# Weaving the output projection of a batch into the next batch's features, first q/k/v projection and score maxima (Trainium2, one core)

## The reference

```python
adj = emb_s * emb_t * softmax(x) / sqrt(n)        # diagonal -inf
x = x + (one where adj is among the 10240 largest of a batch, else zero)
scale, shift = split(cond @ W_emb + b_emb)
xn = rmsnorm(x) * g_norm * (1 + scale) + shift
q, k, v = split(xn @ W_qkv)                       # 16 heads of 64
q, k = rmsnorm(q) * g_q, rmsnorm(k) * g_k
o = softmax(q @ k.T / 8) @ v
x = x + o + o @ W_out
```

## Time and profile before

| | us |
|---|---|
| three runs | 4087.24, 4088.06, 4086.60 (median 4087.24) |
| the profiled execution | 4087.43, of which span 4085.7 |
| PE busy in the span | 3797.2 (93%) |
| DVE, ACT, POOL busy | 2589.9, 1545.2, 1283.3 |
| first A\|B boundary, last values matmul of the batch to the first pair of the next | 1165.88 to 1389.43 |
| the same work in the start, without an old batch | 287.35 to about 450 (features, q/k/v, maxima) |

### The profile page before, as it was taken

The page is one execution under the profiler, slowest core; times in us unless marked ns, Lnnn a source line. Parts: engine busy times, 40 slices in busy tenths (PEclk is TensorE's granted clock), DMA queues, the critical chain, the costliest instruction groups (busy, mean ns, idle before and its releaser), DMA issues.

```text
span 4085.7 us, 44416 instructions
## 1 busy us (share of the span) xinstructions
PE 3797.2 (93%) x16035; PEld 2457.0 (60%) x16035; DVE 2589.9 (63%) x4521; ACT 1545.2 (38%) x2727; POOL 1283.3 (31%) x1907
## 2 busy tenths in 40 slices
PE   5885899999988899999989899999989899999999
PEld 2334666666644667766644677777644677666744
DVE  8996777777774777777774677777775322322221
ACT  1005444444423444444422444444432344444430
POOL 1005433333303533333312533333312433333310
PEclk9996899999998899999999799999999799999999
DMA  4002010000134000010024100000124100000023
GB/s 156 0 15 103 16 37 21 21 21 21 34 133 147 16 21 21 27 31 21 21 101 154 55 21 21 21 21 21 37 71 161 31 21 21 21 21 21 21 81 99
DMA packets 179360, 195.25 MB, mean 48 GB/s; under 512 B 7576, under 2 KB 137680, under 8 KB 178128
## 3 DMA queue, kind: packets, MB, share of 16 engines
q1 hardware_dynamic: 179152, 192.55, 14.9%
HBM read 144.29 MB, written 48.23 MB: 47 GB/s over the span
## 4 chain that ended last, share of the span: by engine, by line
PE 73%; DVE 14%; ACT 5%; POOL 4%; issue 3%; DMA 1%; SPq 0%; DVEq 0%; POOLq 0%; ACTq 0%
PE pax L1003 24%; PE ppv L1072 18%; PE pst L1058 10%; PE pst L991 10%; PE pax L1038 7%; DVE mx L823 3%; DVE xr L718 3%; DVE trash L683 3%; PE pax L1021 2%; POOL xn L379 1%; PE pax L1046 1%; PE pax L1096 1%; ACT sA L545 1%; ACT pt L552 1%; DVE otok L838 1%
## 5 line engine op out<-in xcount | busy, mean ns | idle before, releaser
L1003 PE MATMUL pax<-wh,xn 128*128 128x384 f32 x3840 | 1058.1, 347 | 11.8 <-issue 8.8
L1072 PE MATMUL ppv<-pt,v 128*65 128x512 f32 x2048 | 987.8, 594 | 1.0 <-DVE otok L838 1.0
L683 DVE TENSOR_SCALAR_CACHE_REDUCE trash<-keys,state 128x2048 uint8<-128x2048 f32 x384 | 899.8, 2343 | 9.9
L823 DVE TENSOR_REDUCE mx<-pax 128x1 f32<-128x512 f32 x960 | 617.9, 685 | 222.6 <-PE pax L1038 202.2
L1003 PEld LDWEIGHTS pax<-wh,xn 128*128 128x128 f32 x3840 | 704.7, 189 | 22.9 <-issue 19.6
L552 ACT ACTIVATE pt<-pst 128x1024 f32<-128x1024 f32 x512 | 524.5, 1024 | 503.9 <-PE pst L1058 445.7
L1003 PE MATMUL pax<-wl,xn 128*128 128x384 f32 x1920 | 649.3, 338 | 0.0
L809 DVE TENSOR_REDUCE ss<-sq 128x4 f32<-128x256 f32 x256 | 107.2, 419 | 782.2 <-ACT sq L527 782.2
L1038 PE MATMUL pax<-sA 65*128 65x512 f32 x960 | 473.3, 540 | 28.3 <-ACT sA L540 17.5
L1072 PEld LDWEIGHTS ppv<-pt,v 128*65 128x65 f32 x2048 | 278.5, 137 | 297.2 <-issue 221.7
L351 POOL TENSOR_TENSOR wl<-wf,wh 128x1024 fp32r<-128x1024 f32 x99 | 235.9, 2387 | 586.1 <-ACT wh L468 586.1
(11 more groups left out here) (139 smaller groups left out, 4445.0 us busy)
## 6 DMA issues: line engine op xcount, KB each, us to landing
wf<-in_L_cond_W_qkv SPq DMA_DIRECT2D x99, 512.0 KB, 5.4
keys<-in_x SPq DMA_DIRECT2D x32, 512.0 KB, 8.9
xin<-in_x SPq DMA_DIRECT2D x32, 512.0 KB, 4.0
out_x<-xin SPq DMA_DIRECT2D x32, 512.0 KB, 2.6
wo<-in_L_cond_W_out SPq DMA_DIRECT2D x4, 4096.0 KB, 13.6
pt<-out_x SPq DMA_DIRECT2D x64, 256.0 KB, 3.9
out_x<-pt SPq DMA_DIRECT2D x64, 256.0 KB, 2.5
oT_scr<-ostg SPq DMA_DIRECT2D x56, 256.0 KB, 2.0
```

Source lines behind the costliest of these rows:

```text
L683: e.tensor_scalar(trash[:], kv, thr_f, None, ALU.is_ge, ALU.add, accum_out=cnt[:, c:c + 1]).then_inc(z_cnt, 1)
L823: e.tensor_reduce(mx2[:, j // T, j % T, c:c + 1], max_banks(alone, j)[:, c, :], axis=AX, op=ALU.max).then_inc(m_mx, 1)
L1003: i = e.matmul(qkv_bank(alone, t)[:, 0:6 * DH], xn[:, a, k, t * P:(t + 1) * P], w[:, k, :, :].rearrange("p s c -> p (s c)"), start=(k == 0 ...
L1072: i = e.matmul(ppv[0:DH + 1, c, :], v2[:, par, kt, hh, :], pt[:, kt % 2, c * HALF:(c + 1) * HALF], start=(kt == 0), stop=(kt == T - 1))
```

## The change

- The 16 halves of the projection become calls `project(b, q, lo, hi)` that stand between other work of PE: `last_head` puts q0 to q2 (but for the last head) around the turns of the last head; q3 to q6; q7 one matmul at a time in the first `features`; q8, q9 around the first q/k/v tile; q10 in the second `features`; q11, q12; q13 before the last transposes; q14 and q15 one matmul at a time between the groups of `score_max`. `prep_alone` is gone: all engines run its steps inside `boundary`.
- DVE takes one add per tile beside `finalise_tile` instead of two, and normalises the last head between the ties. Features of rows 512 to 1023 are interleaved with the first two q/k/v tiles.
- `wo`, `xin`, `xr`, `eqm`, `scn` exist twice, by the side of the batch (`side(b)`), and the pair's sides of `sA`, `sB`, `v2` are `(i + b) % 2`, in place of `i % 2`. `xtmp` becomes `xfull`, which holds all columns and shares its place with `xn[:, 1]` (the low part is written over the full one). The halves of `xfull` that are free hold the heads of tiles 0 to 3 until the features reach them; tiles 4 to 7 go to `v2` of the side or to `heads_t`, which now has 128 partitions.
- Row 64 of `sA` is set to -1 once per side and batch (`minus_row`), and is no longer zeroed for each pair: `score_max` contracts over `0:DH`, 64 rows.
- DVE's conditioning in the first boundary comes after its tile 2 instead of 4, and ACT copies the rows of it after its first tile instead of its fourth.
- SP loads the new x first, then the residual; a batch's keys are loaded after all its predecessor's tiles are stored, and the second pair's weights after half 12.

```diff
-    xtmp = sb("xtmp", [P, 2, HALF])
-    wo = sb("wo", [P, KT, N])
...
+    wo = [inner.enter_context(nc.sbuf_tensor(f"wo{r}", [P, KT, N], F32)) for r in range(2)]
...
+    xfull = inner.enter_context(nc.sbuf_tensor("xfull", [P, KT, N], F32))
...
+    xin, xr, eqm, scn = [], [], [], []
+    for r in range(2):
+        xin.append(sb(f"xin{r}", [P, 2, N]))
+        xr.append(sb(f"xr{r}", [P, 4, N]))
+        eqm.append(sb(f"eqm{r}", [P, N]))
+        scn.append(sb(f"scn{r}", [P, N]))
...
+    def side(b):
+
+        return b % 2 if b else 1
...
-    def heads_of(k, t):
-
-        return ostg[:, t * P:(t + 1) * P] if k == KT - 1 else oTt[:, t % 2, k, :]
+    early = xfull[:, 0:KT - 1, HALF:N]
+
+    def late(b, t):
+
+        at = heads_t[:] if t % 2 else v2[:, b % 2].rearrange("p t h d -> p (t h d)")
+        return at[:, 0:(KT - 1) * P].rearrange("p (k c) -> p k c", c=P)
+
+    def heads_of(b, k, t):
+
+        if k == KT - 1:
+            return ostg[:, t * P:(t + 1) * P]
+        return early[:, k, t * P:(t + 1) * P] if t < 4 else late(b, t)[:, k, :]
 
     CST = 2
...
+                e.wait_ge(t_pv, CST + T * 2 * PAIRS * (ob + 1))
+            if fb is not None:
+                self.x_tile(fb, 0)
+                self.x_tile(fb, 1)
...
+                    if t == 1:
+                        self.store_half(ob, 0)
+                    if t > 0:
+                        self.store_half(ob, t)
+            if kb is not None:
+                if ob is not None:
+                    e.wait_ge(t_ot, 2 * PAIRS * (ob + 1))
+                self.load_keys(kb)
...
+                e.dma_start(wo[b % 2][:], w_out.rearrange("(k p) n -> p k n", p=P)).then_inc(d_wo, 16)
+                e.wait_ge(a_qkv, T * PAIRS * (b + 1))
+                e.wait_ge(d_ost, 32 * (PAIRS - 1) * (b + 1) + 16)
+                e.dma_start(early, oT_pairs[:, 0:KT - 1, 0:HALF]).then_inc(d_oe, 16)
+                self.heads_tile(b, 4)
 
...
+
+            e, cols = self.e, slice(g * HALF, (g + 1) * HALF)
+            e.wait_ge(f_ev, 2 * KT * b + KT * g + k + 1)
+            e.tensor_tensor(xn[:, 1, k, cols], xfull[:, k, cols], xn[:, 0, k, cols].bitcast(F32),
+                            ALU.subtract).then_inc(f_lo, 1)
...
+            gp = PAIRS * fb
+            for t in range(4):
+                self.feature_scale(fb, t)
+            for k in range(KT):
+                self.feature_low(fb, 0, k)
+            for t in range(4, 7):
+                self.feature_scale(fb, t)
+            self.prep_tile(gp, 0)
+            self.feature_scale(fb, 7)
+            self.prep_tile(gp, 1)
+            for k in range(KT):
+                self.feature_low(fb, 1, k)
+            self.minus_row(fb, fb % 2)
...
+        def minus_row(self, b, par):
+            e.memset(sA[par][DH:DH + 1, 2:4, :].bitcast(F32), -1.0).then_inc(a_row, 1)
...
             for t in range(T):
-                if fb is not None:
-                    self.finalise_tile(fb, t)
-                    if ob is None and t == T // 2:
-                        self.conditioning()
-                if ob is not None:
-                    self.project_tile(ob, t)
-            if fb is not None:
-                for j in range(2):
-                    e.wait_ge(d_x1[j], 16 * (T // 2) * (fb + 1))
+                self.finalise_tile(fb, t)
+                if ob is None and t == 2:
+                    self.conditioning()
+                if t == 1:
+                    self.add_half(ob, 0)
+                if t > 0:
+                    self.add_half(ob, t)
+            self.add_half(ob, 8)
+            self.prep_sums(gp, 0)
+            self.prep_split(gp, 0)
+            self.add_half(ob, 9)
...
+            self.add_half(ob, 13)
+            self.prep_split(gp, T - 1)
+            for j in range(2 * T):
+                self.row_max(gp, j, True)
+                if j in (6, 13):
+                    self.add_half(ob, 14 + (j > 6))
...
+        def last_head(self, ob, fb):
+
+            e, gp = self.e, PAIRS * ob + PAIRS - 1
+            e.wait_ge(o_wi, ob + 1)
+            e.wait_ge(d_oe, 16 * (ob + 1))
+            self.project(ob, 0, 0, 4)
+            self.out_tokens(gp, 1)
+            self.project(ob, 0, 4, 7)
+            self.project(ob, 1, 0, 7)
+            self.out_rows(gp, 0)
+            if fb is not None:
+                self.before(fb)
+            self.project(ob, 2, 0, 4)
+            self.out_rows(gp, 1)
+            self.project(ob, 2, 4, 7)
+            e.wait_ge(t_oe, 2 * PAIRS * (ob + 1))
+            for q in range(3):
+                self.project(ob, q, 7, 8)
-                    self.project_tile(ob, t, 0)
-                if fb is not None and t == 0:
-                    self.before(fb)
-                    if ob is None:
-                        self.conditioning()
-                if ob is not None:
-                    self.project_tile(ob, t, 1)
-                if fb is not None and t % 4 == 3:
-                    self.features(fb, t // 4)
+                self.last_head(ob, fb)
+            else:
+                self.before(fb)
+                self.conditioning()
+            if fb is None:
+                for q in range(3, 2 * T):
+                    self.project(ob, q)
+                return
+            gp, par = PAIRS * fb, fb % 2
+            for q in range(3, 7):
+                self.project(ob, q)
+            self.features(fb, 0, ob, 7)
+            self.project(ob, 8)
+            self.prep_tile(gp, 0, True)
+            self.project(ob, 9)
+            self.transpose_tile(gp, 0)
+            self.prep_tile(gp, 1, True)
+            self.features(fb, 1, ob, 10)
+            self.project(ob, 11)
+            self.project(ob, 12)
+            self.prep_tile(gp, 2, True)
+            self.transpose_tile(gp, 1)
+            self.prep_tile(gp, 3, True)
+            for t in range(4, T):
+                self.prep_tile(gp, t, True)
+                self.transpose_tile(gp, t - 2)
+            self.transpose_tile(gp, 6)
+            self.project(ob, 13)
+            self.transpose_tile(gp, 7)
+            self.project(ob, 14, 0, 2)
+            for j in range(2 * T):
+                self.score_max(gp, par, j, True)
+                if j == T:
+                    self.max_row(gp, 0)
+                if j < 6:
+                    self.project(ob, 14, j + 2, j + 3)
+                elif j < 13:
+                    self.project(ob, 15, j - 6, j - 5)
+                    if j == 12:
+                        self.project(ob, 15, 7, 8)
 
         def before(self, b):
             e = self.e
...
+                self.project(ob, q, k, k + 1)
+
+        def project(self, b, q, lo=0, hi=KT):
+
+            if b is None:
+                return
+            e, t, c = self.e, q // 2, q % 2
+            if lo == 0:
+                if t >= 4 and c == 0:
+                    e.wait_ge(d_oin[t % 2], 16 * (2 * b + t // 2 - 1))
+                if q >= 4:
+                    e.wait_ge(o_add, 2 * T * b + q - 3)
+            for k in range(lo, hi):
+                i = e.matmul(pst[:, q % 4, :], heads_of(b, k, t), wo[b % 2][:, k, c * HALF:(c + 1) * HALF],
+                             start=(k == 0), stop=(k == KT - 1), skip_group_check=True)
+            if hi == KT:
+                i.then_inc(o_mm, 1)
...
-                e.wait_ge(a_row, 2 * (gp + 1))
+                e.wait_ge(a_row, 2 * (gp // PAIRS) + 1 + (gp % PAIRS > 0))
...
                 elif alone and j > 1 and j != T + 1:
                     e.wait_ge(m_mx, v + c - 3)
-                e.matmul(max_banks(alone, j)[:, c, :], sA[par][0:DH + 1, hh, qt * P:(qt + 1) * P],
-                         sA[par][0:DH + 1, 2 + hh, c * HALF:(c + 1) * HALF], start=True, stop=True).then_inc(m_s, 1)
+                e.matmul(max_banks(alone, j)[:, c, :], sA[par][0:DH, hh, qt * P:(qt + 1) * P],
+                         sA[par][0:DH, 2 + hh, c * HALF:(c + 1) * HALF], start=True, stop=True).then_inc(m_s, 1)
```

More of the change, by code:

```diff
@@ L439, in pair @@
                     self.prep_tile(gp + 1, t)
-            if prep:
+            if prep and gp + 2 < PAIRS * B:
                 self.split_w(gp + 2)
@@ L510, in boundary @@
-            if ob is not None:
-                for c in range(2):
-                    e.wait_ge(d_y[c], 16 * T * (ob + 1))
+            if fb is None:
+                return
+            gp, par = PAIRS * fb, fb % 2
+            for t in range(4):
+                self.feature_rows(fb, t)
+                if ob is None and t == 0:
+                    e.wait_ge(c_cnd, 1)
+                    e.activation(cond_rows.rearrange("b a n -> b (a n)"),
+                                 pst[0:B, :, :].rearrange("b a n -> b (a n)"), ACT.Copy).then_inc(c_rows, 1)
@@ new lines, in boundary @@
+            if ob is None:
+                e.wait_ge(c_cndT, 2)
+            for k in range(KT):
+                self.feature_columns(fb, 0, k)
+            for t in range(4, 7):
+                self.feature_rows(fb, t)
```

(54 more changed lines are left out.)

426 lines of the change are left out of this document (203 added, 223 removed).

## The result

The changed kernel takes 4111.99 us (median of 4 runs, 4111.41 to 4112.92) against 4086.92 of the kernel before beside it: a ratio of 1.0063, with a 95% interval of 1.0045 to 1.0080. It is 25 us slower, where I had forecast 45 faster. The profiled span is 4111.2 us.

What follows compares the result with a forecast made beforehand. PE, busy 93% of the span, was taken as the bound: 4087.4 - 138 (weave) - 3.5 (last boundary) + 6.5 (first boundary) + 90 (64-row maxima) = 4042 us; own range 4005 to 4079, stated range 3946 to 4084.

Steps and rivals of the forecast that it cites:

- part 1: Three batch boundaries: small engines' stages run while PE projects, gaining 46 us each, -138 us in all (-108 to -156).
- 16 matmuls of 0.436 (111.74/256), 7: Woven boundary, between second columns and q/k/v of tile 2: halves 11 and 12 of the projection take 7 us.
- part 4: Pairs' second halves: maxima over 64 rows change the array's form, 0.18 us a change, +3.2 us a pair, +90 in all.
- 2.6 us for x that comes late: Feature chain of a woven boundary: waiting for x adds 2.6 us, as a load takes 4.0 us.
- Rival 3: Boundaries: the weave gives half, since SP's single queue delays each tile some 3 us; 4105 us, chance 0.08.
- 24 us: Maxima stage of a woven boundary, with one projection matmul per two maxima matmuls: 24 us in place of 22.86.
- Part 2: Last boundary: projection halves cover the last head's turn, 2 us of turning matmuls stay; -3.5 us (-2 to -4).
- Part 3: First boundary: features start 8 us later through DVE's wait for ACT's conditioning copy, 1.5 comes back; +6.5 us (0 to 12).
- Rival 1: Maxima over 64 rows: the form costs nothing, or DVE's slack hides the change; 3952 us, chance 0.22.
- rival 2: Pairs' second halves: form changes eat the gain, 0.29 us each, 6.3 us a pair, +176; 4128 us, chance 0.10.
- Part 5: Other edits: two fewer POOL memsets a pair, second buffer copies and early head loads; no term in the sum.
- the pairs' second half at 30 us: Sign in the changed profile: the second half of a pair lasts 30 us instead of 26.7.

## Why the prediction was wrong

**The failed step is part 1, the weave: -138 forecast, -57 measured.** Two things in it were wrong.

*The price of a projection matmul.* "16 matmuls of 0.436 (111.74/256), 7": the 256 of that row are records, and a matmul of full fp32 leaves two. A batch's projection has 16 halves of 8, that is 128 matmuls of 0.87 us. A matmul that is woven in costs the engine twice what I reckoned. That is why the ten matmuls ahead of the ties' sums took 8.64 us and made the chain start 3.4 late (the run with the earlier sums won 2.8 a boundary) and why halves 11 and 12 took 14 us and not 7 between columns and tile 2 (the chain's 14.59 us for 34 records). Half 13 between the last two transposes took 6.95, and two matmuls of half 14 another 1.79; for these the sum of part 1 had no term at all. The run with halves 14 and 15 in front measured the price by itself. The same row served in part 4 for the values ("24 of values"), and did no harm, since I counted records there as well.

*The chain of the features.* "2.6 us for x that comes late" is 7.85 at tile 6 alone, and 3.48 for a residual at tile 2: 8.7 more than the term, where this stage lost 8. Its other terms held; the passes that run beside POOL's low parts were 5.2 us longer, for 5. I priced the load, 4.0 us, and not what asks for it: SP may load tile 6 once ACT has scaled row 4, ACT waits for POOL's scale, and POOL stands in eight low parts, the last seven of which take 16.86 us beside DVE's passes. The scale alone moved ahead of three of them was worth 17.6 us, 11 of them in the woven boundaries. SP's order was worth another 8.9, 11 in the woven boundaries less 2 at the start. Rival 3 named SP's queue and gave 25 us a boundary and 4105: the value was near (19 and 4112), its mechanism was one part of the matter, and 0.08 was too little for it.

The maxima of the boundary, "24 us" from stage start to the pair, also held too little for the changes of form: from first to last 25.8 us against 21.9 with 65 rows, 3.9 of the 4.4.

With 65 rows, the scale, SP's order and the ties' sums mended together the three boundaries win 99 us. What is still short of 138 was not taken apart by a run. An estimate from the chain: halves 11 and 12 cost 7 us more than reckoned, and half 13 with the two matmuls of half 14 8.7, together 16 a boundary or 47 in all, which is enough for it.

**Part 2 was right** in kind, -6.2 for -3.5. The chain has the projection at once behind the last values, in place of the earlier trace rows:

```profile
3996.58 3.43 PE pst L1166 x8
4000.01 0.50 PE ppv L1265 x8
4000.51 8.64 PE pst L1166 x20
4009.15 0.44 PE pax L1277 x4
4009.59 3.44 PE pst L1166 x8
4013.02 0.43 PE pax L1277 x4
4013.46 94.43 PE pst L1166 x220
```

The turning matmuls that stay take 1.4 us of this chain (0.50, 0.44 and 0.43) for the 2 that I let stay, so 4.2 of the 5.6 us went. The 256 records of the projection take 109.9 us of it, where the earlier trace rows has 111.74: the other 1.8, which the forecast did not have.

**Part 3 was right** by its number, +5.7 for +6.5, with some luck, since its reason was only half right: the run with the conditioning moved back shows that its place costs 8 to 11 us, and the one with the earlier scale that 5.5 us could be had there by another edit.

**Part 4 was right** in mechanism and size: 0.19 or 0.14 us a change for 0.18, 2.92 a pair for 3.2, 82 us for 90. That the pause came out at the 0.09 that I took is in part luck: I chose it between two bounds. One reading under them was off: of the loads of L971 the two starts are 0.213 us apart and not 0.195, which makes the pause there 0.14 us and not 0.17. Rival 1 is refuted by the run of the kernel before with 64 rows, rival 2's point of decision (4.8 us a pair) was set by a gain of 135 that was not there: with 57 + 6 - 6 the change was lost from 2 us a pair on.

**Part 5**: nothing contradicts it. That the early loads of heads cost nothing shows in the last chain, where the projection follows the values without a gap.

The expected signs: the pairs' second half at 30 us (29.66) held. The ties' sums under 1.5 (3.77), features 84 us after the start (95), maxima at 155 (174.5) and the first pair at 179 (203.5 by the same mark) did not.

## What to carry to other kernels

Before work is woven into gaps, price one instruction of it by the program's own count, not by the records of the trace, and set that against each gap. Follow each load back to the instruction that permits it, over all engines and queues; in a woven stage the small producer behind a long run of bulk work (a scale behind eight low parts) can set the pace. And where an edit alters the shape of a matmul by a single row, look at its neighbours on the array: here each change of form cost 0.14 to 0.19 us, and an edit that saved POOL two memsets per pair put 31 of them into each.
